# A transformer block and a graph attention on one core: 28 passes of a loop written out, and waits that others imply taken out

## The reference

```python
# layer 0: per sequence b, c = cond[b]
shift_msa, scale_msa, gate_msa, shift_mlp, scale_mlp, gate_mlp = split(silu(c) @ adaln_w + adaln_b, 6)
x_mod = rms(x) * (1 + scale_msa) + shift_msa
q, k, v = split(x_mod @ qkv_w, 3)                  # then RMS norm of q and k per head, rope
attn = softmax(q k^T / 4) v                        # 64 x 64 scores
x = x + gate_msa * (attn @ proj_w + proj_b)
h = rms(x) * (1 + scale_mlp) + shift_mlp
x = x + gate_mlp * ((silu(h @ w1) * (h @ w3)) @ w2)        # 704 hidden
# layer 1: graph attention over the first 20 rows, two directions d
self_feat = concat(x, where(sum(x) == 0, 0, cond)) @ W_self.T + b_self
for d in 0, 1:
    A = adj or its transpose, its first 20 columns
    cond_d, vb = A.sum(-1), A @ w_bias + b_bias
    aff = (self_feat Wq[d] + bq[d]) (kv Wk[d] + bk[d])^T / 4, -9e15 where cond_d <= 0, + vb
    output += (softmax(aff) kv) Wout[d] + bout[d]
x = x + relu(self_feat + output)
```

## Time and profile before

| | us |
|---|---|
| median of 3 runs | 1421.07 |
| lowest, highest run | 1418.9, 1424.15 |
| span of the profiled execution | 1416.1 |
| PE busy | 1342.2 (95%) |
| PEld busy | 1229.1 (87%) |
| DVE busy | 1135.2 (80%) |
| ACT busy | 878.6 (62%) |
| POOL busy | 712.1 (50%) |
| one loop pass, L728 to L728 | 41.4 |

### The profile page before, as it was taken

The page is one execution under the profiler, slowest core; times in us unless marked ns, Lnnn a source line. Parts: engine busy times, 40 slices in busy tenths (PEclk is TensorE's granted clock), DMA queues, the critical chain, the costliest instruction groups (busy, mean ns, idle before and its releaser), DMA issues.

```text
span 1416.1 us, 51305 instructions
## 1 busy us (share of the span) xinstructions
PE 1342.2 (95%) x20276; PEld 1229.1 (87%) x20276; DVE 1135.2 (80%) x2033; ACT 878.6 (62%) x1752; POOL 712.1 (50%) x612
## 2 busy tenths in 40 slices
PE   4679999999999999999999999999999999999985
PEld 3578899999998999999898999999999999999974
DVE  5667888888888888888888888888888888888753
ACT  4556666666666666666666666666666666656542
POOL 0235555455655544555555455555545555554541
PEclk8589999999999999999999999999999999999998
DMA  7001111010111101111110111111011111100100
GB/s 240 29 23 30 45 43 43 18 38 30 43 43 43 43 15 36 34 43 43 43 43 15 35 35 43 43 43 43 15 33 37 43 43 43 43 15 28 30 22 16
DMA packets 49827, 56.19 MB, mean 40 GB/s; under 512 B 4352, under 2 KB 47744, under 8 KB 49792
## 3 DMA queue, kind: packets, MB, share of 16 engines
q1 hardware_dynamic: 48944, 53.86, 12.1%
q10 hardware_dynamic: 848, 1.84, 0.4%
HBM read 47.03 MB, written 8.65 MB: 39 GB/s over the span
## 4 chain that ended last, share of the span: by engine, by line
PE 73%; issue 9%; POOL 7%; ACT 3%; DVE 1%; ACTq 0%; POOLq 0%; DVEq 0%
PE psum L486 39%; PE psum L607 5%; PE psum L622 5%; PE psum L728 4%; PE psum L792 4%; PE psum L758 4%; PE psum L775 3%; POOL nl L1315 3%; PE psum L587 3%; PE psum L806 2%; POOL gl L1315 2%; POOL kbd L1327 2%; ACT gh L926 1%; PE psum L534 1%; ACT qkT L892 1%
## 5 line engine op out<-in xcount | busy, mean ns | idle before, releaser
L1315 POOL TENSOR_TENSOR gl<-gf,gh 128x512 fp32r<-128x512 f32 x96 | 124.3, 1295 | 260.4 <-ACT gh L926 260.4
L486 PE MATMUL psum<-nh,w_lo 128*128 128x256 f32 x704 | 182.2, 289 | 0.0
L486 PE MATMUL psum<-nh,w_hi 128*128 128x256 f32 x704 | 176.8, 282 | 0.0
L1315 POOL TENSOR_TENSOR nl<-xn,nh 128x512 fp32r<-128x512 f32 x64 | 99.2, 1551 | 127.3 <-ACT nh L864 127.3
L486 PEld LDWEIGHTS psum<-nh,w_lo 128*128 128x128 f32 x704 | 132.8, 189 | 1.0 <-issue 1.0
L486 PEld LDWEIGHTS psum<-nh,w_hi 128*128 128x128 f32 x704 | 133.0, 189 | 0.0
L1379 POOL TENSOR_TENSOR e<-e,inv 128x640 f32<-128x640 f32 x64 | 82.0, 1282 | 87.6 <-DVE inv L1271 87.6
L486 PE MATMUL psum<-nl,w_hi 128*128 128x256 f32 x704 | 115.4, 282 | 0.0
L926 ACT ACTIVATE gh<-gf 128x512 fp32r<-128x512 f32 x96 | 60.3, 628 | 61.6 <-DVE gf L1201 60.8
L486 PEld LDWEIGHTS psum<-nl,w_hi 128*128 128x128 f32 x704 | 97.5, 188 | 0.0
L486 PE MATMUL psum<-qkv_lo,nh 128*128 128x512 f32 (+1 forms) x256 | 88.5, 356 | 2.8 <-ACT nh L864 2.8
(11 more groups left out here) (186 smaller groups left out, 4382.4 us busy)
## 6 DMA issues: line engine op xcount, KB each, us to landing
adj<-in_adj SPq DMA_DIRECT2D x32, 440.0 KB, 3.3
x_in<-in_x SPq DMA_DIRECT2D x32, 256.0 KB, 2.7
xn<-in_xT SPq DMA_DIRECT2D x32, 256.0 KB, 3.6
x_res<-in_xT SPq DMA_DIRECT2D x32, 256.0 KB, 3.7
out_T<-y SPq DMA_DIRECT2D x32, 256.0 KB, 2.2
e<-in_adaln ACTq DMA_DIRECT2D x2, 512.0 KB, 5.4
stage<-in_qkv SPq DMA_DIRECT2D x2, 384.0 KB, 5.0
pT<-in_w SPq DMA_DIRECT2D x2, 384.0 KB, 6.4
```

The costliest lines, as they stand in the source:

```text
L486: last = nc.tensor.matmul(out, lhsT, rhs, start=start and i == 0, stop=stop and i == len(terms) - 1)
L1315: return nc.gpsimd.tensor_tensor(out, full, hi.bitcast(F32), ALU.subtract)
```

## The change

1. In `run_steps` the loop becomes `for m in range(1, NM - ahead)`: the 28 middle passes are written out as straight code on each engine, and every wait compares with a constant.
2. `Passes.at_an_end` is set in passes -3 to 0 and 29 to 31. The new `ends_wait`, `ends_wait_last` and `ends_wait_free` issue a wait only there.
3. In the steps, most waits become one of these. What stays in a middle pass are waits that no earlier wait on the same engine implies. A few are moved: `norm1_apply` now waits for `k1_spread` at its second transpose (before, `probs_t` did at its first), `self_feat` waits for `cond_rows_s` at its second output (before, `self_cond` did), and `qkv` gets a wait for `pT_b` or `biased1` at the last of its low-part matmuls of the first half.
4. No arithmetic, no tile and no step's place in `ORDER` is changed.

```diff
+class Passes:
+    at_an_end = True
+def ends_wait(engine, signal, m, n):
+    if Passes.at_an_end:
+        wait(engine, signal, m, n)
+def ends_wait_last(engine, signal, m):
+    ends_wait(engine, signal, m, 0)
+def ends_wait_free(engine, m, *readers):
+    if Passes.at_an_end:
+        wait_free(engine, m, *readers)
...
+    Passes.at_an_end = True
     for m in range(-ahead, 1):
         take(m)
-    with engine.Fori(1, NM - ahead) as m:
+    Passes.at_an_end = False
+    for m in range(1, NM - ahead):
         take(m)
+    Passes.at_an_end = True
     for m in range(NM - ahead, NM):
         take(m)
...
             def norm1_apply(m, n):
                 wait(pe, inverses[1], m, 1)
                 for t in range(TILES):
+                    if t == 1:
+                        wait_free(pe, m, (k1_spread, -1, 4), (qkT_kept, 1, 2))
...
             def score(m, n):
-                wait(pe, qkT_kept, m, TILES)
+                ends_wait(pe, qkT_kept, m, TILES)
                 wait(pe, k_spread, m, TILES)
-                wait_free(pe, m, (g_done, -2, 3), (pT_b, -1, 2))
-                wait_free(pe, m, (down_gated, -2, 1), (v_kept, 0, 2))
-                wait_free(pe, m, (proj_gated, -1, 2), (cos_part, 0, 1))
-                wait_free(pe, m, (row_gate, -2, 1), (cos_part, 0, 2))
+                ends_wait_free(pe, m, (g_done, -2, 3), (pT_b, -1, 2))
+                ends_wait_free(pe, m, (down_gated, -2, 1), (v_kept, 0, 2))
+                ends_wait_free(pe, m, (proj_gated, -1, 2), (cos_part, 0, 1))
+                ends_wait_free(pe, m, (row_gate, -2, 1), (cos_part, 0, 2))
...
             def self_cond(m, n):
                 wait(pe, row_gate, m, 1)
-                wait(pe, cond_rows_s, m, 16)
...
             def score1(m, n):
-                wait(pe, q1_kept, m, ND)
-                wait(pe, k1_spread, m, ND * DC)
+                ends_wait(pe, q1_kept, m, ND)
+                ends_wait(pe, k1_spread, m, ND * DC)
                 wait_free(pe, m, (shifted_s, 2, 2), (g_done, 0, 3))
...
             def score_max(m, t):
-                wait(dve, scores, m, 1)
-                wait(dve, shifted_s, m, t)
+                (ends_wait if t else wait)(dve, scores, m, 1)
+                (wait if t else ends_wait)(dve, shifted_s, m, t)
```

More of the change, by code:

```diff
@@ L557, in qkv @@
                     linear(out, [(nh[0][:, c, rows], w[:, c, cols]) for c in both for w in (wl["qkv"], wh["qkv"])], stop=False)
-                wait(pe, normed_lo[0], m, 1)
+                if t == 0:
+                    wait(pe, normed_lo[0], m, 1)
                 for out, cols in outs:
-                    last = linear(out, [(nl[0][:, c, rows], wh["qkv"][:, c, cols]) for c in both], start=False)
+                    for c in both:
+                        if t == 0 and (out is outs[1][0], c) == (True, 1):
+                            wait_free(pe, m, (pT_b, -1, 2), (biased1, -3, 4))
+                        last = nc.tensor.matmul(out, nl[0][:, c, rows], wh["qkv"][:, c, cols], start=False, stop=c == DC - 1)
                 last.then_inc(qkv_done.sem, 1)
@@ L648, in mlp_up @@
                 first_use(m, "w1", "w3")
-                wait(pe, normed_hi[1], m, 1)
+                (wait if n == 0 else ends_wait)(pe, normed_hi[1], m, 1)
                 chunks = {"w1": [(c, "w1", 2 * n + c) for c in range(2)], "w3": [(c, "w3", 2 * n + c) for c in range(2)]}
@@ L669, in mlp_up @@
                     if name == "w1":
-                        wait(pe, normed_lo[1], m, 1)
+                        (wait if n == 0 else ends_wait)(pe, normed_lo[1], m, 1)
                     for c, w, j in chunks[name]:
@@ L867, in qkv @@
             def qkv(m, t):
[L868 removed]
+                (wait if t else ends_wait)(act, qkv_done, m, t + 1)
                 qk_ps, v_ps = qkv_ps[t]
[L871 removed]
+                (wait if t else ends_wait)(act, qk_sums, m, t)
                 nc.scalar.activation(qk_sq[:, :, :, :].rearrange("p a h f -> p (a h f)"), qk_ps, ACT.Square)\
@@ L902, in probs_t @@
                 wait(act, pT_ps, m, 2 * t + 1)
-                wait(act, mixed, m, t)
+                (wait if t else ends_wait)(act, mixed, m, t)
                 nc.scalar.activation(pT0[:, 0:4, :], pT_out[t][0], ACT.Copy).then_inc(pT_a.sem, 1)
@@ L985, in probs_t1 @@
                 wait(act, pT1_ps, m, 2 * t + 1)
-                wait(act, mixed1, m, t)
+                (wait if t else ends_wait)(act, mixed1, m, t)
                 nc.scalar.activation(pT1[:, 0:4, :], pT1_out[t][0], ACT.Copy).then_inc(pT1_a.sem, 1)
@@ L1115, in qkv @@
                 wait(dve, qk_squares, m, t + 1)
-                wait(dve, rotated, m, 2 * t)
+                (wait if t else ends_wait)(dve, rotated, m, 2 * t)
                 qk_ps = qkv_ps[t][0].rearrange("p (a h f) -> p a h f", a=2, f=DH)
@@ L1137, in rope @@
             def rope(m, t):
-                wait(dve, rotated, m, 2 * t + 2)
-                wait(dve, qk_inverses, m, 1)
+                ends_wait(dve, rotated, m, 2 * t + 2)
+                (ends_wait if t else wait)(dve, qk_inverses, m, 1)
                 q_v = qr[t][:, :, :, :].rearrange("p a h f -> p (a h) f")
@@ L1188, in mlp_up @@
                 wait(dve, z_tanh, m, n + 1)
-                wait(dve, g_lo, m, n)
-                wait(dve, g_hi, m, n)
+                (wait if n else ends_wait)(dve, g_lo, m, n)
+                ends_wait(dve, g_hi, m, n)
                 if 2 * n + 1 < MC - 1:
@@ L1199, in mlp_up @@
                 wait(dve, z_silu, m, n + 1)
-                wait(dve, z_done, m, 2 * n + 2)
+                (wait if 2 * n + 1 < MC - 1 else ends_wait)(dve, z_done, m, 2 * n + 2)
                 nc.vector.tensor_tensor(gf[:, :, :], gf[:, :, :], u_ps[n], ALU.mult).then_inc(g_done.sem, 1)
@@ L1243, in score1_bias @@
             def score1_bias(m, t):
-                wait(dve, scores1, m, 1)
-                wait(dve, edge_ready, m, 1)
-                wait(dve, pT1_ps, m, 2 * (t + 1 - TILES))
+                (ends_wait if t else wait)(dve, scores1, m, 1)
+                ends_wait(dve, edge_ready, m, 1)
+                ends_wait(dve, pT1_ps, m, 2 * (t + 1 - TILES))
                 for a in range(ND):
@@ L1324, in heads @@
             def heads(m, t):
-                wait(pool, qkT_kept, m, t + 1)
-                wait_last(pool, scores, m)
+                (ends_wait if t else wait)(pool, qkT_kept, m, t + 1)
+                ends_wait_last(pool, scores, m)
                 nc.gpsimd.tensor_tensor(kbd[:, t, :, :, :, :].rearrange("p c s h k -> p (c s) h k"),
```

161 lines of the change are left out of this document (79 added, 82 removed).

## The result

The change takes 1428.0 us (median of 15 runs, 1426.04 to 1432.38) where before takes 1422.15 (1416.63 to 1427.07). The ratio is **1.0042**, interval 1.0031 to 1.0054: slower by about 6 us, inside the 0.5% that was set as no change. 1444 had been forecast, with "slower by over 0.5%" as the likeliest case: the sign was right and the size was not.

A forecast was written before the change was run, and what follows sets the result against it. PE, busy 95% of the span, was taken as the bound. Span 1416.1 − 11.8 (waits) + 35.4 (late code) − 0.7 (first loop pass's break) = 1439.0, plus 5.0 around it: 1444 us, worked out as 1436 to 1459, range given 1405 to 1462.

The forecast's parts named there:

- the boundaries at x of 200 and more: Code-block boundary at instruction x of L775 (score1): stalls 0.92, 1.30, 1.72, 1.68 us for x = 200, 216, 232, 248.
- The two breaks: PE stalls in L775's loads before the change: 2.34 us in pass 0 (x = 230), 0.81 in first loop pass (202).
- (c): Rival: shorter PE stalls because blocks are asked for earlier; 0.4 of the size, 14.2 us, time 1423; chance 0.12.
- The rest of the series: PE stalls in L775 and L758 for boundaries x = 8 to 184: from 1.92 down to 0.16 us a pass.
- From entering a block to using the next: PE's code fetch: taken as 3.5 us, with 3.8 as other end; PE stalls when a block lasts less.
- What the waits gave back: Removed waits and control instructions in a middle pass: 0.42 us a pass, between 0.18 and 0.60; 11.8 us over 28.
- The wait of L607: PE's wait for DVE's L1248 at L607 goes as DVE's chain gets shorter: 0.24 us a pass.
- The gate's row: Gate matmuls and L587, between self_cond and score: 0.10 + 0.08 = 0.18 us a pass gained; DVE's gate wait remains.
- What had been put at 0: Other real waits stay, including the k1_spread wait in norm1_apply and moved cond_rows_s wait; bounded at 0.05 either way.
- (a): Rival: the code fetch is hidden, so PE has no stalls; 1408.6 us, by the bound 1403; chance 0.20.
- (b): Rival: PE's clock falls after breaks of 1.5 us or more, 12 passes at 1.5 more each; 1462 us; chance 0.16.
- (d): Rival: the change does not do what it says; given nothing, as no PE control instruction is left in middle passes.

The follow-up runs named there:

- e3: The change with 16 satisfied waits added to PE per middle pass among the MLP matmuls, holding the code boundary at instruction 232; 1406.84 us, 0.9881 of before; again 0.9909.
- e5: e3 with six of its 16 added PE instructions moved among the transposes ahead of score1, boundary at 226; 1481.76 us, one run.
- e2: The kernel before with only its loop written out as straight code, all waits kept; 1460.11 us, 1.0244 of before.
- e1: The change with its middle passes put back into a loop of 28 turns on every engine, few waits kept; 1413.59 us, 0.9949 of before.
- e7: The change with PE's middle passes in a loop and those of the other engines written out; 1406.01 us, 0.9892 of before.
- e11: e7 with PE keeping all the waits of its end passes in its loop too; 1413.68 us, one run.
- e4: e3 with the 16 added waits beginning only in the sixth middle pass, so the boundary stays at instruction 56; 1451.01 us, 1.0204 of before.
- e6: The change with its middle passes in a loop of 14 turns, two passes per body (2553 PE instructions); 1497.59 us, one run.

## Why the prediction was wrong, step by step

**The step that failed** is the one for the boundaries at x of 200 and more, "there the two breaks measure the cost". Its six passes were put at 9.0 us and cost none. The two breaks were taken in passes in which control instructions of PE stand close ahead of `score1`; the change leaves none in a middle pass. The sequencer is then far enough ahead that in all six passes the packet comes 2.4 to 2.7 us ahead of the step. In the change's pass 1 (x = 232), for which 1.72 was forecast:

```profile
162.87 1.40 PEld L806 LDWEIGHTS psum<-kbd,q1T 32*64 32x64 f32 x128 [0.17 <-issue]
164.31 1.76 PEld L789 LDWEIGHTS psum<-wo,kv 128*32 128x32 f32 x64
```

and its DMA busy tenths from 160 to 166 us (slices of 0.15; the packet of PE's code among the first, and the next at 164.8):

```profile
DMA  4140000000000000000000000000000040000000
```

e3 shows the same 28 times, e5 shows that six control instructions bring the break back, and e2, which keeps those of before, has breaks of 1.12 to 2.37 there. The prediction had this as its rival (c), "blocks are asked for earlier because no wait holds the sequencer", but argued against it from a window in which nothing was waited for, and gave it to all breaks alike. It applied only where the block that is entered begins ahead of `score1`.

**The rest of the series held**, with one exception. Measured is the pass less 40.82:

| x | forecast | measured, first time and sixteen passes later |
|---|---|---|
| 8 | 1.92 | 0.69, 0.73 |
| 24 | 1.78 | 1.81, 2.09 |
| 40 | 1.65 | 1.42, 1.53 |
| 56 | 1.52 | 1.74, 2.11 |
| 72 | 1.45 | 1.17, 1.02 |
| 88 | 1.33 | 1.51, 1.32 |
| 104 | 1.15 | 1.13, 1.28 |
| 120 | 1.03 | 1.01, 1.13 |
| 136 | 0.65 | 0.69, 0.41 |
| 152 | 0.48 | 0.30, 0.37 |
| 168, 184 | 0.33, 0.16 | 0.16, 0.22 |
| 200, 216 | 0.92, 1.30 | 0.00, 0.01 |
| 232 | 1.72 | 0.04, −0.02 |
| 248 | 1.68 | −0.02, 0.02 |

From 24 to 184 the 20 passes were put at 22.6 us and took 22.4, break for break at load (x + 256)/2 of `score1` and `v1`, with a period of 16 passes. From entering a block to using the next the breaks show 3.0 to 3.9 us, where 3.5 had been taken. The two at x = 8 took 1.4 instead of 3.8: there the sequencer's lead still helps. The DMA busy tenths of pass 3 from 242.5 to 248.5 us (slices of 0.15; `score1` starts at 244.53):

```profile
DMA  0000000000003000000000000000000000400000
```

The packet comes at 244.35, 0.2 us ahead of the step, where at x = 24 it comes 1.0 behind it (pass 4). In all 23.9 instead of 35.4.

**What the waits gave back** was mis-sized: 0.42 us a pass forecast (0.18 to 0.60), 0.59 measured (41.41 to 40.82), 16.5 us instead of 11.8. The wait of L607 went as forecast, about 0.20 against 0.24 by how much earlier that step starts in the pass; e1 and e7 show that it needs DVE's straight code, which is what pass 0 had been compared for. The gate's row in the change is

```profile
195.46 0.29 PEld L511 LDWEIGHTS psum<-gate,cond_rows 8*128 8x128 f32 x2 [0.23 <-DVE gate L1241]
195.88 0.96 PEld L617 LDWEIGHTS psum<-kbd,qkT 32*64 32x64 f32 x64
```

with starts 0.42 apart instead of 0.52, the 0.10 of the control instruction, and 0.23 of idle time that DVE's `gate` ends, about what pass 0 had shown: 0.18 in all, as forecast. What had been put at 0 is what was missed: `score1` starts 0.17 us earlier behind `k1` than before. e11, which keeps PE's waits, has 0.12 of it, and e1, a loop with few waits, all of it. So most of it comes from the other engines' waits and not from PE's register instruction there. Which work comes earlier is not shown.

**The sum.** Forecast: 35.4 − 11.8 − 0.7 = 22.9. In the profiled executions the 28 middle passes are 7.0 longer, 23.9 − 16.5 − 0.4 (before's first loop pass is 0.7 over 41.41 and its last 0.2 under it), and 2.3 more lie outside them, for the span's 9.3. Pass 30 is 1.1 longer, 0.9 of it a break of the same kind after load 55 of `v1`; the work behind it is 2.0 longer, and what lies ahead of the middle passes 0.9 shorter. At the end the granted clock of the change is lower (0.50 for 24.6 us in the last two stretches, 14.9 in all there before), and no run here says why. The medians are 5.9 apart.

**The rivals.** (a), the fetch is hidden: refuted as a whole by e4, and true at x of 200 and more; its time, 1408.6 (1403 by the bound), is near what e3 (1406.84) and e7 (1406.01) take. (b), the falling clock: real in e2 and in 18 passes of e5, and absent in the middle passes of the change, whose longest break is 1.78. That its breaks were too short is not shown to be the reason: the clock fell behind 1.42 in e5 and 1.66 in e4, and stayed at the full level behind 2.44 in e2. (c) came nearest to the time, 1423 for stalls of 0.4 of the size; they were 0.67 of it, and the larger gain did the rest, so that its time is near is in part luck. (d) is excluded by the profile: breaks, packets and shorter clean passes are all there.

Of what was to be seen, the packets (158 for 160), the step of 8 loads, the period of 16 and L607's wait came true. The pass lengths (41.0 and 42.7) were 40.8 and 42.9.

## What to carry to other kernels

Read how many instructions of an engine a pass of the loop has and how fast its densest step issues them: where 256 instructions pass in less than the 3.0 to 3.9 us that lay here between entering a block and using the next, straight code can stall that engine, and how much depends on where a block ends and on what stands ahead of it, so an edit of a few instructions elsewhere can move the time by tens of us. Keep such an engine in a loop whose body is held, and write out those whose chains are slowed by register instructions (e7, 1.1% faster than before). And when a cost is taken from a rare place in the trace, such as the first passes, look at what is special there before it is carried to all others.

## What the runs showed of the hardware

- Control instructions of PE, even with satisfied waits, that stand among the transposes ahead of `score1` delay the next block: with six of them the packet came 0.9 us behind the start of the step instead of 2.6 ahead of it (e5, e3), and 25 of 28 passes broke. The same kind of instructions among the 256-column matmuls of the MLP cost nothing (e3 and the clean passes of the change: 40.83 and 40.82).
- A loop body of 1279 or 1312 instructions of PE is held, one of 2553 is fetched anew each turn, with 2.89 to 3.26 us at the branch (e1, before, e6).
- Behind a break of 2.37 us the granted clock stayed at 0.50 for some 9 us (e2), and that pass was 6.6 us over the shortest; it fell too behind one of 1.42 (e5) and one of 1.66 (e4), and did not behind one of 2.44 (e2), three of 2.01 to 2.22 (e5) and all of the change's middle passes, up to 1.78. So the length of a break alone does not decide it.
